# An attention kernel on one core: the threshold masks in one arithmetic form on GpSimd, and two divisions taken off VectorE's reads of PSUM

## The chip, the cores and the metric

The kernel runs on one core of one Trainium2 chip. The metric is the device time of one execution in microseconds (us). Before the change the median of three runs is 1256.25 us (1255.8 to 1259.92).

## The reference, cut to what matters

32 batches of 256 tokens with 128 channels, 16 heads of 8 channels. Each batch passes a layer norm, a query/key/value product, a layer norm of each head's queries and keys, and then two attentions, which are mixed and projected (D is 8, and topk is 12 of 256 keys):

```python
scores = jnp.einsum('bhnd,bhmd->bhnm', q, k) / jnp.sqrt(jnp.float32(D))
aw = jax.nn.softmax(scores, axis=-1)
kth = jax.lax.top_k(aw, topk)[0][..., -1:]
mask = (aw >= kth).astype(aw.dtype)
aws = aw * mask
aws = aws / (aws.sum(-1, keepdims=True) + 1e-08)
o_s = jnp.einsum('bhnm,bhmd->bhnd', aws, v)
qf = jax.nn.softmax(q, axis=-1)
kf = jax.nn.softmax(k, axis=-1)
kv = jnp.einsum('bhnd,bhne->bhde', kf, v)
z = jnp.einsum('bhnd,bhd->bhn', qf, kf.sum(axis=2))
o_l = jnp.einsum('bhnd,bhde->bhne', qf, kv) / (z[..., None] + 1e-06)
o = a * o_s + (1.0 - a) * o_l
return o @ Wproj.T + bproj
```

## The kernel before

Each engine runs its own program, written out by hand, and the engines meet only at semaphores. The loop over batches (`it`) is software-pipelined: iterations -2 to 3 and 28 to 33 are written out, and between them runs a hardware loop whose body holds four batches. In an iteration every engine goes through eight units `u_` = 0 to 7, one for each pair of heads. A unit holds four tiles of 128 queries by 256 keys.

The sparse attention of one unit passes through the engines so:

- TensorE writes the scores of unit u+1 to `score_ps` (`scores`).
- VectorE takes the 8 largest of each row (`top`, L539) and GpSimd subtracts the maximum (`drop`, L371).
- ScalarE takes the exponentials (`e`, L724, with row sums in `z`), and those of the eight largest (`e8`, L729).
- VectorE, a unit later, removes the eight largest (`rest`, L546) and takes the next eight (`next`, L552). The fourth of these is the threshold.
- Two units after that unit's scores, the mask `below` is made: by GpSimd for some of the four tiles (L393, the table `POOL_TILES` = 3, 2, 3, 4, 4, 4, 3, 2) and by ScalarE for the others (L737).
- TensorE (`turn`, L841 and L842) transposes `e` and adds `below` times -2^40 in the same PSUM tile, and ScalarE copies it through a ReLU (`kept`, L694), which leaves only what passes the threshold. TensorE multiplies with the values (`product`, L862), four heads at a time, and ScalarE copies `oT` (L746).

Once a batch there is other work in fixed units. For the linear attention TensorE multiplies in unit 2 (L958, result in `work_ps`: 32 groups of 8 sums and a divisor), and VectorE in unit 3 takes the reciprocals of the divisors (`lin_z`, L567) and the products (`lin`, L570), both from PSUM. In unit 5 TensorE turns the sparse sums of the previous batch into `pv_ps` (`sums`, L873), and VectorE makes `den` (L586), its reciprocal (L591) and `o_sparse` (L594). TensorE may write `work_ps` anew (L968) when `lin` is there, and `pv_ps` (L862 of unit 6) when `o_sparse` is there. Other once-a-batch work of VectorE: statistics (L602, L608), `kv` (L560), `d_max` (L578), `k_rec` (L611). GpSimd's: the norms of queries and keys (L336 to L358, L381), `d_sub` (L401), `k_half`, `k_quarter` and `k_sum` (L422), `k_feat` (L429).

The queries and keys of the next batch go through DRAM. ScalarE writes three bf16 parts (`part`, L708 in unit 4, L758 in units 4 and 5), SyncE stores them (L274) and loads them as `q_slots` and `k_slots` (L281). TensorE needs them for the scores of the next batch's unit 0, at the end of unit 7.

In `extra(u_, k)` of VectorE, `k` tells the place between the removals and searches of a unit.

## Time and profile before

| what | value |
|---|---|
| median of three runs | 1256.25 us |
| the profiled execution, its own time | 1254.07 us |
| its span in the trace | 1252.3 us |
| VectorE (DVE) busy | 1187.9 us, 95% |
| ScalarE (ACT) busy | 1086.6 us, 87% |
| GpSimd (POOL) busy | 1083.9 us, 87% |
| TensorE (PE) busy | 972.0 us, 78% |
| granted TensorE clock, mean | 0.959 |

Busy time is the time in which an engine had an instruction under way. Short instructions of VectorE and ScalarE overlap: the next one starts before the one ahead has ended. So what an instruction costs on a full engine is the distance from its start to the next one's start, which the timeline gives, and not its own duration. A wait stands in brackets behind the instruction that waited, with the releaser.

### The profile page before, as it was taken

What the parts mean: (1) busy time and instruction counts of PE and PEld (TensorE: products, weight loads), DVE (VectorE), ACT (ScalarE), POOL (GpSimd) and SP (SyncE); (2) the same over time, 40 slices, a digit from 0 to 9 for tenths busy, and PEclk for the clock granted to TensorE, in tenths of its full rate; (3) what the DMA queues carried; (4) which work ended last, traced back from release to release, by engine and by line L of the source; (5) the groups of instructions that cost most, each with busy time, mean ns of one, the idle gap of its engine ahead of it and who ended that gap; (6) DMA issues with size and microseconds to landing.
All of it is one profiled execution on the core that took longest, in us unless ns stands there. A gap on an engine that the chain in (4) does not pass through costs nothing.

```text
span 1252.3 us, 38772 instructions
## 1 busy us (share of the span) xinstructions
PE 972.0 (78%) x8997; PEld 655.4 (52%) x9028; DVE 1187.9 (95%) x4553; ACT 1086.6 (87%) x3626; POOL 1083.9 (87%) x1688
## 2 busy tenths in 40 slices
PE   2578788887788777877877888788868788877876
PEld 0245555555455554555545555455545555555554
DVE  7699999999899998999989999899989999999994
ACT  2498999999799997999979899799988999999984
POOL 4598999999899997999979999799988999999974
PEclk9999999899899998999989999899999998999998
DMA  2122221212221222221122221122221222222110
GB/s 61 47 73 78 81 80 40 70 57 82 83 82 43 66 69 72 82 81 54 55 59 82 82 81 51 48 69 82 82 84 36 67 63 82 81 81 71 41 52 14
DMA packets 165211, 83.45 MB, mean 67 GB/s; under 512 B 7753, under 2 KB 164943, under 8 KB 164946
## 3 DMA queue, kind: packets, MB, share of 16 engines
q1 hardware_dynamic: 164946, 80.56, 22.4%
q8 instruction: 88, 1.44, 0.5%
q14 instruction: 177, 1.45, 0.4%
HBM read 42.78 MB, written 37.75 MB: 64 GB/s over the span
## 4 chain that ended last, share of the span: by engine, by line
DVE 53%; issue 32%; DVEq 6%; PE 5%; POOL 2%; ACT 1%; SPq 0%; DMA 0%; POOLq 0%; ACTq 0%
DVE rest L546 22%; DVE top L539 18%; DVE next L552 8%; DVEq L75 5%; POOL below L393 2%; PE turn_ps L841 1%; PE pv_ps L862 1%; DVE o_sparse L594 1%; DVE lin_z L567 1%; PE turn_ps L842 1%; ACT e L724 1%; DVE stats L602 0%; DVE den L586 0%; DVE x_mv L608 0%; DVE lin L570 0%
## 5 line engine op out<-in xcount | busy, mean ns | idle before, releaser
L393 POOL TENSOR_SCALAR below<-e,next 128x256 bf16<-128x256 f32 x800 | 724.6, 922 | 0.2 <-issue 0.2
L724 ACT ACTIVATE e<-score_ps,drop 128x256 f32<-128x256 f32 x1024 | 473.2, 481 | 53.8 <-POOL drop L371 51.3
L841 PE MATMUL turn_ps<-ident,e 128*128 128x128 f32 x2048 | 406.5, 292 | 61.9 <-issue 22.4
L546 DVE MATCH_REPLACE8 rest<-e 128x256 f32<-128x256 f32 x1024 | 409.8, 402 | 0.0
L552 DVE MAX8 next<-rest 128x8 f32<-128x256 f32 x1024 | 402.9, 406 | 0.0
L539 DVE MAX8 top<-score_ps 128x8 f32<-128x256 f32 x1024 | 358.8, 408 | 31.5 <-issue 16.9
L842 PE MATMUL turn_ps<-minus_huge,below 128*128 128x128 bf16 x2048 | 383.9, 226 | 0.0
L841 PEld LDWEIGHTS turn_ps<-ident,e 128*128 128x128 f32 x2048 | 300.3, 147 | 107.2 <-issue 62.2
L694 ACT ACTIVATE kept<-turn_ps 128x1024 f32<-128x1024 f32 x256 | 267.6, 1045 | 68.1 <-PE turn_ps L842 67.8
L842 PEld LDWEIGHTS turn_ps<-minus_huge,below 128*128 128x128 bf16 x2048 | 224.9, 110 | 0.2
L724 ACT ACTIVATION_READ_ACCUMULATOR e<-score_ps,drop 128x1 f32 x1024 | 217.6, 213 | 0.0
L862 PE MATMUL pv_ps<-kept,v_aug 128*32 128x256 f32 x2048 | 145.5, 404 | 1.9 <-ACT out_sb L770 1.3
L371 POOL TENSOR_TENSOR drop<-top 128x36 f32<-128x36 f32 x256 | 62.8, 245 | 82.3 <-DVE top L539 81.7
L823 PE MATMUL score_ps<-k_slots,q_slots 64*128 64x256 bf16 x1024 | 104.7, 282 | 19.4 <-ACT e L724 11.1
L737 ACT ACTIVATE below<-e,next 128x256 bf16<-128x256 f32 x224 | 108.2, 516 | 0.0
L862 PEld LDWEIGHTS pv_ps<-kept,v_aug 128*32 128x32 f32 x2048 | 55.6, 113 | 49.5 <-issue 29.5
L823 PEld LDWEIGHTS score_ps<-k_slots,q_slots 64*128 64x128 bf16 x1024 | 31.0, 95 | 79.8 <-issue 72.8
L939 PE MATMUL work_ps<-w_qk,xnT 128*128 128x256 f32 x128 | 46.8, 448 | 31.6 <-ACT xnT L786 31.6
L546 DVE MATCH_VALUE_LOAD rest<-e 128x8 f32 x1024 | 68.4, 67 | 0.8 <-ACT e L729 0.8
L729 ACT ACTIVATE e<-drop 128x32 f32<-128x32 f32 x256 | 63.4, 248 | 0.0
L873 PE MATMUL pv_ps<-gather,oT 128*128 128x128 f32 x256 | 35.0, 280 | 29.4 <-ACT oT L746 29.2
L958 PE MATMUL work_ps<-kv,qfT 128*128 128x144 f32 x128 | 25.3, 322 | 35.1 <-DVE kv L560 35.1
(156 smaller groups left out, 1333.0 us busy)
## 6 DMA issues: line engine op xcount, KB each, us to landing
part_slots<-part SPq DMA_DIRECT2D x128, 192.0 KB, 2.3
q_slots<-part_slots SPq DMA_DIRECT2D x64, 256.0 KB, 3.4
k_slots<-part_slots SPq DMA_DIRECT2D x64, 256.0 KB, 4.0
part_slots<-part SPq DMA_DIRECT2D x64, 128.0 KB, 2.0
x_sb<-in_L_attn_x SPq DMA_DIRECT2D x32, 128.0 KB, 4.0
x_res<-in_L_attn_x SPq DMA_DIRECT2D x32, 128.0 KB, 3.9
out_y<-out_sb SPq DMA_DIRECT2D x32, 128.0 KB, 4.4
w_ops<-in_L_ffn_W SPq DMA_DIRECT2D x1, 512.0 KB
```

Of the source, the lines that this page charges most:

```text
L393: nc.gpsimd.tensor_scalar(below[:, r, t, :], e[:, r, t, :], next8[:, r, t, TOPK - 9:TOPK - 8], None, ALU.is_lt).then_inc(s["below_pool"], 1)
L539: nc.vector.max(top[:, q, t, 1:9], score_ps[:, q, t // 2, t % 2, :]).then_inc(s["top_ready"], 1)
L546: nc.vector.match_replace(rest[:, t, :], e8[:, (u_ - 1) % 2, t, :], e[:, (u_ - 1) % RING, t, :], REMOVED).then_inc(s["rest_ready"], 1)
L552: nc.vector.max(next8[:, (u_ - 1) % RING, t, :], rest[:, t, :]).then_inc(s["next_ready"], 1)
L694: nc.scalar.activation(kept[:, u_ % 4], turn_ps[:], ACT.Relu).then_inc(s["turn_copied"], 1)
L724: nc.scalar.activation(e[:, u_ % RING, t, :], score_ps[:, u_ % 2, t // 2, t % 2, :], ACT.Exp, bias=drop[:, u_ % 2, t, 0:1], accum_out=z[:, ...
L729: nc.scalar.activation(e8[:, u_ % 2], drop[:, u_ % 2, :, 1:9], ACT.Exp).then_inc(s["e8_ready"], 1)
L737: nc.scalar.activation(below[:, r, t, :], e[:, r, t, :], ACT.Relu, scale=-1.0, bias=next8[:, r, t, TOPK - 9:TOPK - 8]).then_inc(s["below_a ...
L823: last = mm(score_ps[:, v_ % 2, hh, nt, :], q_slots[rows, side, v_, nt * P:(nt + 1) * P], k_slots[rows, side, v_, :], start=True, stop=True)
L841: mm(dst, e[:, r, t, keys], ident[:], start=True, stop=False, is_transpose=True)
L842: last = mm(dst, below[:, r, t, keys], minus_huge[:], start=False, stop=True)
L862: last = mm(pv_ps[32 * j:32 * (j + 1), 0:N], v_aug[:, side, mc, 4 * q + j, :], kept[:, v_ % 4, j % 2, mc, :], start=(mc == 0), stop=(mc == ...
```

## The change

All four tiles of every unit's mask are made by GpSimd, no longer by comparing but as min(e - threshold, 0). The result is at most zero, so the matrix that TensorE multiplies it with changes its sign (`huge` for `minus_huge`). ScalarE makes no masks any more, and TensorE waits for one semaphore in place of two.

Both divisions are split in four steps. ScalarE copies the 288 columns from PSUM (`lin_raw` in unit 3, ahead of that unit's exponentials; `sums_sb` in unit 5, behind them). VectorE takes only the reciprocals, from SBUF (`lin_z` in unit 4, `den` in unit 7). GpSimd multiplies (`lin` in unit 4, `o_sparse` in unit 7) and forms the denominator of the sparse part in unit 6. TensorE may write the PSUM tiles anew once ScalarE has copied them.

```diff
-POOL_TILES = (3, 2, 3, 4, 4, 4, 3, 2)
...
+                    if u_ == 6 and exists(it - 1):
+                        wait_alone(pool, s["sums_copied"], it, s["waits_passed"])
+                        nc.gpsimd.tensor_scalar(den[:, 0], z[:, nxt].rearrange("p t h -> p (t h)"), SUM_EPS, None,
+                                                ALU.mult).then_inc(s["den_step"], 1)
+                        pool.wait_ge(s["den_step"], it)
+                        nc.gpsimd.tensor_tensor(den[:, 1], den[:, 0], sums_sb[:, :, D], ALU.add).then_inc(
+                            s["den_ready"], 1)
...
-                        for t in range(POOL_TILES[r]):
+                        for t in range(TILES):
                             wait_alone(pool, s["next_ready"], TILES * (g - 2) + t + 1, s["waits_passed"])
                             nc.gpsimd.tensor_scalar(below[:, r, t, :], e[:, r, t, :],
-                                                    next8[:, r, t, TOPK - 9:TOPK - 8], None,
-                                                    ALU.is_lt).then_inc(s["below_pool"], 1)
+                                                    next8[:, r, t, TOPK - 9:TOPK - 8], 0.0,
+                                                    ALU.subtract, ALU.min).then_inc(s["below_ready"], 1)
...
+                    if u_ == 4 and exists(it):
+                        pool.wait_ge(s["linz_ready"], it + 1)
+                        nc.gpsimd.tensor_tensor(lin[:, par].rearrange("p t (h d) -> p (t h) d", d=D),
+                                                lin_raw[:, :, 0:D],
+                                                lin_z[:].unsqueeze(2).to_broadcast([P, NT * H, D]),
+                                                ALU.mult).then_inc(s["lin_ready"], 1)
...
+                    if u_ == 7 and exists(it - 1):
+                        pool.wait_ge(s["rden_ready"], it)
+                        nc.gpsimd.tensor_tensor(o_sparse[:].rearrange("p t (h d) -> p (t h) d", d=D),
+                                                sums_sb[:, :, 0:D],
+                                                den[:, 2].unsqueeze(2).to_broadcast([P, NT * H, D]),
+                                                ALU.mult).then_inc(s["osp_ready"], 1)
...
-                    if u_ == 3 and k in (1, 3) and exists(it):
-                        w = work_ps[:, 0:NT * H * VA].rearrange("p (t h e) -> p t h e", t=NT, e=VA)
-                        if k == 1:
-                            dve.wait_ge(s["w_lin"], it + 1)
-                            nc.vector.reciprocal(lin_z[:], w[:, :, :, D]).then_inc(s["linz_step"], 1)
-                        if k == 3:
-                            dve.wait_ge(s["linz_step"], it + 1)
-                            nc.vector.tensor_tensor(
-                                lin[:, par].rearrange("p t (h d) -> p (t h) d", d=D),
-                                work_ps[:, 0:NT * H * VA].rearrange("p (g e) -> p g e", e=VA)[:, :, 0:D],
-                                lin_z[:].rearrange("p t h -> p (t h)").unsqueeze(2).to_broadcast([P, NT * H, D]),
-                                ALU.mult).then_inc(s["lin_ready"], 1)
...
-                    if u_ == 5 and 1 <= k <= 4 and exists(it - 1):
-                        w = pv_ps[:, 0:NT * H * VA].rearrange("p (g e) -> p g e", e=VA)
-                        n = 2 * (it - 1)
-                        if k == 1:
-                            dve.wait_ge(s["w_turn"], it)
-                            nc.vector.scalar_tensor_tensor(out=den[:, 0], in0=z[:, nxt].rearrange("p t h -> p (t h)"),
-                                                           scalar=SUM_EPS, in1=w[:, :, D], op0=ALU.mult,
-                                                           op1=ALU.add).then_inc(s["den_step"], 1)
-                        if k == 2:
-                            dve.wait_ge(s["den_step"], n + 1)
-                            nc.vector.reciprocal(den[:, 1], den[:, 0]).then_inc(s["den_step"], 1)
-                        if k == 4:
-                            dve.wait_ge(s["den_step"], n + 2)
-                            nc.vector.tensor_tensor(o_sparse[:].rearrange("p t (h d) -> p (t h) d", d=D), w[:, :, 0:D],
-                                                    den[:, 1].unsqueeze(2).to_broadcast([P, NT * H, D]),
-                                                    ALU.mult).then_inc(s["osp_ready"], 1)
+                    if u_ == 4 and k == 1 and exists(it):
+                        dve.wait_ge(s["lin_copied"], it + 1)
+                        nc.vector.reciprocal(lin_z[:], lin_raw[:, :, D]).then_inc(s["linz_ready"], 1)
+                    if u_ == 7 and k == 1 and exists(it - 1):
+                        dve.wait_ge(s["den_ready"], it)
+                        nc.vector.reciprocal(den[:, 2], den[:, 1]).then_inc(s["rden_ready"], 1)
...
+                    if u_ == 3 and exists(it):
+                        act.wait_ge(s["w_lin"], it + 1)
+                        wait(act, s["lin_ready"], it)
+                        nc.scalar.copy(lin_raw[:].rearrange("p g e -> p (g e)"), work_ps[:, 0:NT * H * VA]).then_inc(
+                            s["lin_copied"], 1)
...
-                        for t in range(POOL_TILES[r], TILES):
-                            nc.scalar.activation(below[:, r, t, :], e[:, r, t, :], ACT.Relu, scale=-1.0,
-                                                 bias=next8[:, r, t, TOPK - 9:TOPK - 8]).then_inc(s["below_act"], 1)
...
+                    if u_ == 5 and exists(it - 1):
+                        act.wait_ge(s["w_turn"], it)
+                        wait(act, s["osp_ready"], it - 1)
+                        nc.scalar.copy(sums_sb[:].rearrange("p g e -> p (g e)"), pv_ps[:, 0:NT * H * VA]).then_inc(
+                            s["sums_copied"], 1)
...
-                    pe.wait_ge(s["below_pool"], POOL_SUM * batch + POOL_UPTO[r + 1])
-                    wait(pe, s["below_act"], (UNITS * TILES - POOL_SUM) * batch + TILES * (r + 1) - POOL_UPTO[r + 1])
+                    pe.wait_ge(s["below_ready"], TILES * (g2 + 1))
...
-                                last = mm(dst, below[:, r, t, keys], minus_huge[:], start=False, stop=True)
+                                last = mm(dst, below[:, r, t, keys], huge[:], start=False, stop=True)
...
-                        wait(pe, s["osp_ready"], it)
+                        wait(pe, s["sums_copied"], it)
...
-                        wait(pe, s["lin_ready"], it + 1)
+                        wait(pe, s["lin_copied"], it + 1)
```

VectorE, units 3 and 4 of one iteration, before (the lines L546, L552 and L539 are the removals, the searches for the next eight and for the first eight):

```order
L539 MAX top<-score_ps 128x8 x4
L546 MATCH_REPLACE rest<-e 128x256 x2
L567 RECIPROCAL lin_z<-work_ps 128x32
L552 MAX next<-rest 128x8
L546 MATCH_REPLACE rest<-e 128x256
L570 TENSOR_TENSOR lin<-work_ps,lin_z 128x256
L552 MAX next<-rest 128x8
L546 MATCH_REPLACE rest<-e 128x256
L552 MAX next<-rest 128x8
L578 TENSOR_REDUCE d_max<-qkn 128x64
L552 MAX next<-rest 128x8
L539 MAX top<-score_ps 128x8 x4
```

The same place in the changed kernel (its line numbers are others: L560, L567 and L573 are those three):

```order
L560 MAX top<-score_ps 128x8 x4
L567 MATCH_REPLACE rest<-e 128x256 x2
L573 MAX next<-rest 128x8
L567 MATCH_REPLACE rest<-e 128x256
L573 MAX next<-rest 128x8
L567 MATCH_REPLACE rest<-e 128x256
L573 MAX next<-rest 128x8
L586 TENSOR_REDUCE d_max<-qkn 128x64
L573 MAX next<-rest 128x8
L560 MAX top<-score_ps 128x8 x4
```

The reciprocal and the product have left unit 3. One reciprocal, from SBUF, stands in unit 4, behind these rows.

GpSimd, units 6 and 7, before:

```order
L371 TENSOR_TENSOR drop<-top 128x36
L393 TENSOR_SCALAR below<-e,next 128x256 x4
L371 TENSOR_TENSOR drop<-top 128x36
L393 TENSOR_SCALAR below<-e,next 128x256 x4
L429 TENSOR_TENSOR k_feat<-k_exp,k_rec 128x256
```

And in the changed kernel:

```order
L370 TENSOR_TENSOR drop<-top 128x36
L386 TENSOR_SCALAR den<-z 128x32
L389 TENSOR_TENSOR den<-den,sums_sb 128x32
L400 TENSOR_SCALAR below<-e,next 128x256 x4
L370 TENSOR_TENSOR drop<-top 128x36
L400 TENSOR_SCALAR below<-e,next 128x256 x4
L442 TENSOR_TENSOR o_sparse<-sums_sb,den 128x256
L450 TENSOR_TENSOR k_feat<-k_exp,k_rec 128x256
```

Three instructions have come in, two of them ahead of the masks of unit 6. In these two units GpSimd made all four tiles before, too.

## Rows read from the trace of the kernel before

**Rows 1.** The page, part 1: busy time of each engine.

```profile
PE 972.0 (78%) x8997; PEld 655.4 (52%) x9028; DVE 1187.9 (95%) x4553; ACT 1086.6 (87%) x3626; POOL 1083.9 (87%) x1688
```

**Rows 2.** Busy time by stretch: PE, PEld, DVE, ACT, POOL, then clock and DMA.

```profile
100.00:300.00 200.00, 166.08 (x1560) 112.56 (x1564) 199.16 (x767) 185.94 (x622) 184.12 (x289) 0.97 0.27 76
```

**Rows 3.** Waits of VectorE: total us, times, longest.

```profile
DVE top L539 <- issue: 16.9, 5, 3.6
DVE top L539 <- PE score_ps L823: 13.6, 8, 5.7
DVE den L586 <- PE pv_ps L873: 12.6, 2, 12.0
```

**Rows 4.** Timeline of TensorE, one batch apart: start, us, what.

```profile
520.98 0.70 PE L939 MATMUL work_ps<-w_qk,xnT 128*128 128x256 f32 x2 [1.04 <-ACT xnT L786]
...
557.32 0.70 PE L939 MATMUL work_ps<-w_qk,xnT 128*128 128x256 f32 x2 [1.04 <-ACT xnT L786]
```

**Rows 5.** Timeline of VectorE in unit 3, around the linear part.

```profile
613.12 0.34 DVE L567 RECIPROCAL lin_z<-work_ps 128x32 f32<-128x32 f32 x1
613.38 0.36 DVE L552 MAX8 next<-rest 128x8 f32<-128x256 f32 x1
...
614.05 0.40 DVE L570 TENSOR_TENSOR lin<-work_ps,lin_z 128x256 f32<-128x256 f32 x1
614.38 0.41 DVE L552 MAX8 next<-rest 128x8 f32<-128x256 f32 x1
```

**Rows 6.** Timeline of VectorE in unit 5, around the sparse part.

```profile
622.66 0.17 DVE L586 SCALAR_TENSOR_TENSOR den<-z,pv_ps 128x32 f32<-128x32 f32 x1
622.76 0.41 DVE L552 MAX8 next<-rest 128x8 f32<-128x256 f32 x1
623.09 0.32 DVE L591 RECIPROCAL den<-den 128x32 f32<-128x32 f32 x1
623.35 0.02 DVE L546 MATCH_VALUE_LOAD rest<-e 128x8 f32 x1
...
624.02 0.39 DVE L594 TENSOR_TENSOR o_sparse<-pv_ps,den 128x256 f32<-128x256 f32 x1
624.34 0.07 DVE L546 MATCH_VALUE_LOAD rest<-e 128x8 f32 x1
```

**Rows 7.** Timeline of VectorE in unit 6, around a reciprocal from SBUF.

```profile
629.28 0.32 DVE L611 RECIPROCAL k_rec<-k_sum 128x32 f32<-128x32 f32 x1
629.53 0.36 DVE L552 MAX8 next<-rest 128x8 f32<-128x256 f32 x1
```

**Rows 8.** Groups of GpSimd, shapes apart: busy us, mean ns, idle before.

```profile
L393 POOL TENSOR_SCALAR below<-e,next 128x256 bf16<-128x256 f32 x800 | 724.6, 922 | 0.2 <-issue 0.2
...
L429 POOL TENSOR_TENSOR k_feat<-k_exp,k_rec 128x256 f32<-128x256 f32 x32 | 20.1, 630 | 0.5 <-DVE k_rec L611 0.5
L338 POOL TENSOR_SCALAR qk_rsqrt<-qk_rsqrt 128x64 f32<-128x64 f32 x32 | 7.9, 247 | 6.4 <-POOL qk_rsqrt L336 6.4
L412 POOL TENSOR_SCALAR x_shift<-x_shift 128x2 f32<-128x2 f32 x32 | 7.5, 235 | 6.4 <-POOL x_shift L409 6.4
L338 POOL TENSOR_SCALAR x_rsqrt<-x_rsqrt 128x2 f32<-128x2 f32 x32 | 6.1, 191 | 6.4 <-POOL x_rsqrt L336 6.4
```

**Rows 9.** Groups of ScalarE, the same columns.

```profile
L737 ACT ACTIVATE below<-e,next 128x256 bf16<-128x256 f32 x224 | 108.2, 516 | 0.0
L746 ACT COPY oT<-pv_ps 128x256 f32<-128x256 f32 x128 | 49.1, 384 | 1.7 <-PE pv_ps L862 1.7
```

**Rows 10.** Timeline, units 6 to 0: the load, the scores, VectorE's search.

```profile
592.07 0.51 SPq L281 DMA_DIRECT2D k_slots<-part_slots  x1
...
595.65 0.40 PE L823 MATMUL score_ps<-k_slots,q_slots 64*128 64x256 bf16 x4
...
597.67 1.40 DVE L539 MAX8 top<-score_ps 128x8 f32<-128x256 f32 x4
```

**Rows 11.** Timeline of GpSimd at the end: the last nine masks.

```profile
1227.80 8.10 POOL L393 TENSOR_SCALAR below<-e,next 128x256 bf16<-128x256 f32 x9
```

More of the change, by code:

```diff
@@ L57 @@
 ROWS = len(SLOTS) * D
-POOL_TILES = (3, 2, 3, 4, 4, 4, 3, 2)
-POOL_SUM = sum(POOL_TILES)
-POOL_UPTO = tuple(sum(POOL_TILES[:v]) for v in range(UNITS + 1))
 RING = 8
@@ L112, in build @@
         ident = sb("ident", [P, P])
-        minus_huge = sb("minus_huge", [P, P], BF16)
+        huge = sb("huge", [P, P], BF16)
         minus_one = sb("minus_one", [P, P], BF16)
@@ L177, in build @@
         qfT = sb("qfT", [P, N])
-        lin_z = sb("lin_z", [P, NT, H])
+        lin_raw = sb("lin_raw", [P, NT * H, VA])
+        lin_z = sb("lin_z", [P, NT * H])
         lin = sb("lin", [P, 2, NT, C])
@@ L194, in build @@
         oT = sb("oT", [P, 2, QUADS, N])
-        den = sb("den", [P, 2, NT * H])
+        sums_sb = sb("sums_sb", [P, NT * H, VA])
+        den = sb("den", [P, 3, NT * H])
         o_sparse = sb("o_sparse", [P, NT, C])
@@ L206, in build @@
             scores_ready top_ready rest_ready next_ready drop_ready e8_ready waits_passed
-            exp_done below_pool below_act turn_ready turn_copied pv_ready pv_copied
+            exp_done below_ready turn_ready turn_copied pv_ready pv_copied
             x_stats x_mean x_rsqrt_step x_rsqrt_ready x_newton xn_ready
@@ L211, in build @@
             dmax_ready dsub_ready dexp_ready ksum_step ksum_ready krec_ready feat_ready
-            w_v_ready v_copied w_kv kv_ready w_qfT qfT_copied w_lin linz_step lin_ready
-            w_turn den_step osp_ready w_osT osT_copied w_out y_ready""".split()
+            w_v_ready v_copied w_kv kv_ready w_qfT qfT_copied w_lin lin_copied linz_ready lin_ready
+            w_turn sums_copied den_step den_ready rden_ready osp_ready w_osT osT_copied w_out y_ready""".split()
         s = {n: sem(n) for n in names}
@@ L296, in _ @@
             select(ident[:], ALU.not_equal, 1.0, 0, [[-1, P]], 1, 1).then_inc(s["ident_ready"], 1)
-            nc.gpsimd.memset(minus_huge[:], 0.0).then_inc(s["pool_step"], 1)
+            nc.gpsimd.memset(huge[:], 0.0).then_inc(s["pool_step"], 1)
             nc.gpsimd.memset(own_head[:], 1.0).then_inc(s["pool_step"], 1)
@@ L301, in _ @@
             nc.gpsimd.memset(v_aug[:], 0.0).then_inc(s["pool_step"], 1)
-            select(minus_huge[:], ALU.not_equal, -HUGE, 0, [[-1, P]], 1, 4).then_inc(s["pool_const"], 1)
+            select(huge[:], ALU.not_equal, HUGE, 0, [[-1, P]], 1, 4).then_inc(s["pool_const"], 1)
             select(own_head[:], ALU.is_ge, 0.0, 0, [[-D, H], [0, VA]], 1, 4).then_inc(s["pool_step"], 1)
@@ L718, in body @@
                         if u_ == 0:
-                            wait(act, s["osp_ready"], it - 1)
+                            wait(act, s["den_ready"], it - 1)
                         wait(act, s["turn_ready"], g - RING + 1)
@@ L729, in body @@
                         nc.scalar.activation(e8[:, u_ % 2], drop[:, u_ % 2, :, 1:9], ACT.Exp).then_inc(s["e8_ready"], 1)
-                    if exists(it if u_ >= 2 else it - 1):
-                        r = (u_ - 2) % RING
-                        act.wait_ge(s["next_ready"], TILES * (g - 1))
-                        for t in range(POOL_TILES[r], TILES):
-                            nc.scalar.activation(below[:, r, t, :], e[:, r, t, :], ACT.Relu, scale=-1.0,
-                                                 bias=next8[:, r, t, TOPK - 9:TOPK - 8]).then_inc(s["below_act"], 1)
                     if u_ % 2 == 0 and exists(it if u_ >= 6 else it - 1):
@@ L830, in turn @@
                     r = (u_ - 4) % RING
-                    batch = it if u_ >= 4 else it - 1
-                    pe.wait_ge(s["below_pool"], POOL_SUM * batch + POOL_UPTO[r + 1])
-                    wait(pe, s["below_act"], (UNITS * TILES - POOL_SUM) * batch + TILES * (r + 1) - POOL_UPTO[r + 1])
+                    pe.wait_ge(s["below_ready"], TILES * (g2 + 1))
                     wait(pe, s["turn_copied"], g2)
```

## The prediction, on record before the changed kernel ran

> **What bounds the kernel now.** I read busy times first, then a stretch of the steady part, then VectorE's waits, and last the timeline between the instructions that the change touches. Over the whole span VectorE leads with 95%, and ScalarE and GpSimd follow with 87% each [rows 1]; from this alone any of the three could be the limit. The steady stretch decides: from 100 to 300 us VectorE is busy for 199.16 of 200 us, GpSimd for 184.12 and ScalarE for 185.94 [rows 2]. So in the steady part VectorE never waits, and the other two do. VectorE's list of waits says the same: in the whole execution it has three large entries, 16.9, 13.6 and 12.6 us [rows 3]. The 16.9 us are five stops of up to 3.6 us in front of the first search of a unit, in which the profile sees nothing waited for. Each lies before the first search of an iteration whose number is a multiple of four: they are the jumps back to the head of the loop. The 12.6 us are the drain after the last batch. Of the 13.6 us, 5.7 lie in one wait at the start, the others mostly just behind those jumps. A batch takes 557.32 - 520.98 = 36.3 us [rows 4], and 32 of them make 1163 of the 1252 us. Whatever shortens VectorE's program in a batch shortens the batch, as long as the others follow.
>
> **VectorE, what leaves and what comes.** VectorE's instructions overlap, so I take the distance from a start to the next start.
> - Linear part: `lin_z` 613.38 - 613.12 = 0.26 us, `lin` 614.38 - 614.05 = 0.33 us [rows 5].
> - Sparse part: `den` 622.76 - 622.66 = 0.10 us, its reciprocal 623.35 - 623.09 = 0.26 us, `o_sparse` 624.34 - 624.02 = 0.32 us [rows 6].
> - These leave: 0.26 + 0.33 + 0.10 + 0.26 + 0.32 = 1.27 us a batch.
> - Two reciprocals of 32 elements from SBUF come in. `k_rec` is exactly that, and its slot is 629.53 - 629.28 = 0.25 us [rows 7], so 0.50 us come.
>
> Net 0.77 us a batch, 32 times: 24.6 us, of which the last batch's sparse part doesn't count, since it lies in the drain. I take 24.0 us. By the instructions' own durations (0.34 + 0.40 + 0.17 + 0.32 + 0.39 less 0.64, so 0.98 us a batch) it would be 31 us, but those count overlapped time twice.
>
> **GpSimd, the unknown price.** The old mask costs 922 ns a tile [rows 8], or 8.10 / 9 = 0.90 us from start to start [rows 11]. The trace has no tile with subtract and min, so I bound it. The form with two arithmetic operations exists at 64 and at 2 elements: 247 and 191 ns [rows 8], which is (247 - 191) / 62 = 0.90 ns an element. At 256 elements that gives 191 + 254 x 0.90 = 420 ns. This is my lower bound. The upper bound is the comparison's own 922 ns: if what makes it dear is the threshold read from memory, or the bf16 output, both of which stay, nothing gets cheaper. The row with one operation (235 ns at 2 elements against 191 with two) shows that leaving out the second operation does not make an instruction cheaper [rows 8]. I take 0.45 us, near the lower end, since the two rows with the same pair form are the nearest in operation, and leave the upper end to a rival.
>
> The new work: two products of 256 elements at the 630 ns of `k_feat`, and two operations of 32 elements at some 240 ns, between the 235 and the 247 of the two small rows [rows 8]: 1.74 us a batch. All other work of GpSimd is 1083.9 - 724.6 = 359.3 us, or 11.2 us a batch [rows 1, 8]. With 32 masks at 0.45 us that is 11.2 + 1.7 + 14.4 = 27.3 us, against a batch of 36.3 - 0.8 = 35.5 us. GpSimd has room. It becomes the bound when 32 masks take more than 35.5 - 12.9 = 22.6 us, so at 0.71 us a mask.
>
> The row for the old mask works out at (922 - 191) / 254 = 2.9 ns an element, three times the pair form's [rows 8]. The Trainium skill (GPSIMD Engine Reference, section 3.1) gives bodies of at most two operations 1.03 cycles an element and a tight loop without branches some 1.8 cycles at best, and section 7 gives bodies that make a boolean 2.03 cycles unless unrolled. By its figures, at the 1.2 GHz that it states, an estimate for the new mask is 0.2 to 0.4 us plus the fixed part, so 0.4 to 0.6 us; the sum would stay as it is, since that lies under the 0.71 us that decide. The rows agree with the page on the direction, not on the comparison's size.
>
> **ScalarE.** 224 masks of 516 ns go, 108.2 us of busy time, and 64 copies of 288 columns come, at `oT`'s 384 ns for 256 columns some 0.4 us each, 26 us [rows 9]. Net 82 us less, of 1086.6 [rows 1]. It was not the bound, so this gives nothing by itself. Locally it is not all relief: in unit 5 ScalarE made no masks (all four were GpSimd's), and now the copy of `sums_sb` stands ahead of the last part cast. The copy of `lin_raw` stands ahead of the exponentials of unit 3. It waits for the product out of `kv`, which TensorE issues in unit 2, while those exponentials wait for VectorE's search in unit 3; so it should be hidden.
>
> **The new waits.** VectorE in unit 4 waits for a copy made in unit 3, and in unit 7 for a denominator that GpSimd forms near the head of unit 6. Each has about a unit of some 4.5 us (36.3 / 8) to arrive [rows 4]. Behind them on VectorE stand the searches that everything waits for, so a late one would cost in full. GpSimd's masks of unit 6 stand behind the wait for `sums_copied`, and TensorE needs these masks only two units after that. TensorE's waits for `work_ps` and `pv_ps` now end with a copy in place of the division; the one comes earlier, the other at about the same place in the unit.
>
> **Start, jumps, drain.** The stops at the jumps (16.9 us) and the waits behind them (some 7.5 us of the 13.6) [rows 3] don't come from work that the change touches, and I leave them. In the drain GpSimd's last nine masks take 8.10 us [rows 11] and would take 4 us or less, but TensorE's turns and ScalarE's copies then pace it; I give that 1 to 2 us of gain. Against it the last division becomes a chain of copy, two small operations, reciprocal and product, 0.4 + 0.5 + 0.3 + 0.6 = 1.8 us where 1.0 us stood, with two more handovers. The two cancel.
>
> **The sum.** 1254.07 - 24.0 = 1230.1 us for an execution like the profiled one. That one was 2.2 us under the median, so against the median 1256.25 - 24 = 1232 us.
>
> **Rivals.**
> - *A, VectorE stays full and the batch shrinks by 0.77 us*: 1232 us, own range 1225 to 1239. For it: 199.16 of 200 us, and a batch in which nobody else is over 93% busy. Chance 0.62.
> - *B, the mask is not cheap, and GpSimd becomes the bound* (slower). From 0.71 us a mask on. At 0.90 us a batch takes 11.2 + 1.7 + 28.8 = 41.7 us, 5.4 more than now, 32 times 173 us: about 1430 us. At 0.80 us it is 38.5 us, and 1325 us. For it: 922 ns is the only row with this size, this scalar from memory and this output; against it the slope of the pair form. Chance 0.17.
> - *C, the gain goes into a new wait*. The place to look is the round through DRAM: the last part is cast in unit 5, stored and loaded (issued at 592.07), the scores start at 595.65 and end 0.4 us later, and VectorE searches them at 597.67 [rows 10]. The margin is 1.6 us. VectorE now gets from unit 5 to unit 0 faster by 0.68 - 0.25 = 0.43 us, and the cast comes 0.35 to 0.4 us later behind the new copy. That takes half the margin. If the margin fell short by all of the 0.77 us, the time would be the old 1256 us; between, 1245 to 1256. Chance 0.12.
> - *D, more than the sum*: shorter queues on GpSimd and ScalarE also shorten the waits behind the jumps and the start, by up to those 7.5 us and the drain's 2 us [rows 3]: 1216 to 1224 us. Chance 0.09.
>
> The Trainium skill (GPSIMD Engine Reference, section 4.1) advises against GpSimd for elementwise work, which it puts at about half VectorE's speed with two inputs. The rows agree on the ratio's direction: 630 ns for `k_feat` against 0.33 us for the `lin` slot [rows 5, 8]. Alone it would speak against the move; it counts only on an engine without room, and then it is rival B.
>
> **How the numbers follow.** The likeliest is A, 1232 us. The range from 1216 to 1256 holds A, C and D, 0.83 together; B lies outside. About 0.3% (3.8 us) is what a measurement of this kernel can tell from no change. Faster than that are A, D and a part of C (0.04): 0.75. Within it, the rest of C less a little: 0.07. Slower: B, and 0.01 of C: 0.18.
>
> **What would show it.** Right if a batch lasts some 35.5 us and VectorE is still busy for over 99% of the steady stretch, with its busy total some 24 to 31 us lower; if the mask group on GpSimd has a mean under 0.6 us and GpSimd falls to some 70%; if the five stops at the jumps stay. Wrong if the waits of VectorE list new entries at the reciprocals or at the searches of unit 0, or if GpSimd's masks have TensorE's turns and then the searches wait.

## The result: 1654 us, a third slower

The changed kernel takes 1654.2 us (median of 4 runs, 1653.39 to 1655.17) against 1256.03 us (1253.92 to 1259.92): a ratio of 1.317, 95% interval [1.313, 1.320]. The prediction was 1232 us.

The page of the changed kernel, part 1, and its stretch from 100 to 300 us (the columns of [rows 1, 2]):

```profile
PE 1173.5 (71%) x8997; PEld 773.1 (47%) x9028; DVE 1195.5 (72%) x4457; ACT 1032.3 (62%) x3466; POOL 1558.8 (94%) x2040
100.00:300.00 200.00, 144.17 (x1121) 94.81 (x1122) 147.08 (x550) 128.42 (x431) 194.36 (x253) 0.80 0.18 51
```

VectorE has fallen from 199.16 to 147.08 of 200 us [rows 2], and GpSimd leads with 194.36. The other engines follow. TensorE is busy for 144.17 of the 200 us in place of 166.08 [rows 2], and its granted clock is 0.80 on average in place of 0.97, so it spends part of the time at the lower of its two levels (1.2 of 2.4 GHz). GpSimd's group for the masks stands at the head of part 5 of the page:

```profile
L400 POOL TENSOR_SCALAR below<-e,next 128x256 bf16<-128x256 f32 x1024 | 1151.3, 1146 | 0.0
```

That is 1146 ns a mask where the comparison took 922 ns [rows 8], and 1024 of them where there were 800. The batch and the way in which GpSimd holds up the others, in timelines: VectorE (two rows, one batch apart), then GpSimd, then ScalarE and VectorE together:

```profile
708.92 0.69 DVE L586 TENSOR_REDUCE d_max<-qkn 128x64 f32<-128x512 f32 x1 [2.16 <-POOL qkn L357]
...
758.84 0.69 DVE L586 TENSOR_REDUCE d_max<-qkn 128x64 f32<-128x512 f32 x1 [2.17 <-POOL qkn L357]
```

```profile
719.43 0.19 POOL L337 TENSOR_SCALAR x_rsqrt<-x_rsqrt 128x2 f32<-128x2 f32 x1 [0.20 <-POOL x_rsqrt L335]
...
720.58 0.63 POOL L424 TENSOR_TENSOR lin<-lin_raw,lin_z 128x256 f32<-128x256 f32 x1
721.16 0.24 POOL L370 TENSOR_TENSOR drop<-top 128x36 f32<-128x36 f32 x1
721.39 4.50 POOL L400 TENSOR_SCALAR below<-e,next 128x256 bf16<-128x256 f32 x4
```

```profile
719.76 1.41 DVE L560 MAX8 top<-score_ps 128x8 f32<-128x256 f32 x4
721.44 0.47 ACT L728 ACTIVATE e<-score_ps,drop 128x256 f32<-128x256 f32 x1 [2.47 <-POOL drop L370]
723.67 0.09 DVE L567 MATCH_VALUE_LOAD rest<-e 128x8 f32 x1 [2.50 <-ACT e L733]
```

A batch takes 758.84 - 708.92 = 49.9 us instead of 36.3 [rows 4]. `drop`, a small subtraction, stands in GpSimd's queue behind masks and products; ScalarE's exponentials wait for it, and VectorE's removals for the exponentials. The waits in sum (us, times, longest), ScalarE's in the first row:

```profile
ACT e L728 <- POOL drop L370: 392.6, 217, 4.0
DVE rest L567 <- ACT e L733: 273.2, 198, 2.5
DVE d_max L586 <- POOL qkn L357: 66.1, 31, 2.3
DVE top L560 <- issue: 22.3, 6, 4.9
```

In the chain that ended last (part 4 of the page) the masks alone have nearly half:

```profile
POOL below L400 46%; POOL drop L370 3%; ACT e L728 3%; POOLq L72 2%; POOL qkn L357 2%; POOL d_sub L408 2%; DVE rest L567 2%; DVE top L560 2%; POOL sq_half L380 1%; POOL o_sparse L442 1%; PE pv_ps L859 1%; POOL k_feat L450 1%; DVE next L573 1%; POOL k_half L436 1%; POOL sq_quarter L380 1%
```

### The profile page after: what moved, and what is told of

Same layout as the page of the kernel before. It is cut to its first block, busy times and chain, and to the rows that moved or that the text cites. A ratio compares the mean times of both kernels' runs of the same rounds, so it can differ in the third digit from the quotient of the medians.

```text
span 1653.0 us, 38768 instructions
## 1 busy us (share of the span) xinstructions
PE 1173.5 (71%) x8997; PEld 773.1 (47%) x9028; DVE 1195.5 (72%) x4457; ACT 1032.3 (62%) x3466; POOL 1558.8 (94%) x2040
## 3 DMA queue, kind: packets, MB, share of 16 engines
q1 hardware_dynamic: 164946, 80.56, 16.9%
## 4 chain that ended last, share of the span: by engine, by line
POOL 61%; issue 23%; DVE 5%; ACT 3%; PE 3%; POOLq 3%; DMA 1%; DVEq 1%; SPq 0%; ACTq 0%
POOL below L400 46%; POOL drop L370 3%; ACT e L728 3%; POOLq L72 2%; POOL qkn L357 2%; POOL d_sub L408 2%; DVE rest L567 2%; DVE top L560 2%; POOL sq_half L380 1%; POOL o_sparse L442 1%; PE pv_ps L859 1%; POOL k_feat L450 1%; DVE next L573 1%; POOL k_half L436 1%; POOL sq_quarter L380 1%
## 5 line engine op out<-in xcount | busy, mean ns | idle before, releaser
L400 POOL TENSOR_SCALAR below<-e,next 128x256 bf16<-128x256 f32 x1024 | 1151.3, 1146 | 0.0
L838 PE MATMUL turn_ps<-ident,e 128*128 128x128 f32 x2048 | 484.9, 329 | 101.3 <-POOL below L400 89.8
L839 PE MATMUL turn_ps<-huge,below 128*128 128x128 bf16 x2048 | 453.3, 250 | 0.0
L838 PEld LDWEIGHTS turn_ps<-ident,e 128*128 128x128 f32 x2048 | 347.3, 170 | 175.2 <-POOL below L400 89.7
L567 DVE MATCH_REPLACE8 rest<-e 128x256 f32<-128x256 f32 x1024 | 415.0, 408 | 0.0
L573 DVE MAX8 next<-rest 128x8 f32<-128x256 f32 x1024 | 407.4, 411 | 0.6
L560 DVE MAX8 top<-score_ps 128x8 f32<-128x256 f32 x1024 | 361.3, 415 | 55.5 <-PE score_ps L822 32.4
L567 DVE MATCH_VALUE_LOAD rest<-e 128x8 f32 x1024 | 79.9, 78 | 274.0 <-ACT e L733 273.2
L839 PEld LDWEIGHTS turn_ps<-huge,below 128*128 128x128 bf16 x2048 | 251.2, 123 | 0.7
L859 PE MATMUL pv_ps<-kept,v_aug 128*32 128x256 f32 x2048 | 175.0, 470 | 92.0 <-ACT sums_sb L747 90.8
L909 PE MATMUL pv_ps<-x_res,ident 128*128 128x128 f32 x128 | 32.8, 344 | 79.6 <-issue 79.2
L370 POOL TENSOR_TENSOR drop<-top 128x36 f32<-128x36 f32 x256 | 63.9, 250 | 12.3 <-DVE top L560 12.3
L965 PE MATMUL work_ps<-ident,qkn 128*128 128x128 f32 x128 | 31.6, 395 | 54.0 <-POOL qkn L357 53.9
L586 DVE TENSOR_REDUCE d_max<-qkn 128x64 f32<-128x512 f32 x32 | 21.9, 685 | 66.1 <-POOL qkn L357 66.1
L909 PEld LDWEIGHTS pv_ps<-x_res,ident 128*128 128x128 f32 x128 | 23.4, 228 | 86.6 <-issue 85.7
```

Of the source, the lines that this page charges most:

```text
L370: nc.gpsimd.tensor_tensor(drop[:, q], top[:, q], top[:, q, :, 1:2].to_broadcast([P, TILES, 9]), ALU.subtract).then_inc(s["drop_ready"], 1)
L400: nc.gpsimd.tensor_scalar(below[:, r, t, :], e[:, r, t, :], next8[:, r, t, TOPK - 9:TOPK - 8], 0.0, ALU.subtract, ALU.min).then_inc(s["bel ...
L560: nc.vector.max(top[:, q, t, 1:9], score_ps[:, q, t // 2, t % 2, :]).then_inc(s["top_ready"], 1)
L567: nc.vector.match_replace(rest[:, t, :], e8[:, (u_ - 1) % 2, t, :], e[:, (u_ - 1) % RING, t, :], REMOVED).then_inc(s["rest_ready"], 1)
L573: nc.vector.max(next8[:, (u_ - 1) % RING, t, :], rest[:, t, :]).then_inc(s["next_ready"], 1)
L838: mm(dst, e[:, r, t, keys], ident[:], start=True, stop=False, is_transpose=True)
```

## Experiments

The theory after the result: (1) min(e - threshold, 0) is a dear form on GpSimd, and (2) with all masks there, GpSimd paces the batch. Rivals: what makes it dear is the bf16 output or the threshold in memory; the divisions' new waits do a part of it. Later there was a second question: where VectorE's 24 us went.

**1. What a form costs (m1_forms, m2_forms).** The kernel before, with further instructions of GpSimd behind its last batch, four of each form; their results aren't used. Each of the two ran once. In m1_forms:

```diff
+            def f_pair_memory_bf16(i):
+                return nc.gpsimd.tensor_scalar(probe_b[:, i, :], one, thr, 0.0, ALU.subtract, ALU.min)
...
+            def f_multadd_memory_f32(i):
+                return nc.gpsimd.tensor_scalar(probe_f[:, i, :], one, thr, 1.5, ALU.mult, ALU.add)
```

> The kernel before, and behind its last mask GpSimd runs 14 forms of instruction, four times each (one of them on 1024 elements, three on shorter rows). Known: comparison with the threshold from memory, bf16 out: 922 ns; subtract and min with the threshold from memory: 1146 ns. Theory 1, the scalar from memory is what costs: with an immediate both fall to 420 to 500 ns, and multiply-add with a scalar from memory rises to 900 to 1150. Theory 2, the bf16 output costs: with f32 out both fall under 600 ns. Theory 3, the number and kind of operations cost, whatever the operands: subtract and min stays at 1100 to 1150 in every variant, one operation (comparison, min, subtract) at 900 to 950. Theory 4, only the small rows misled me (a fixed part hides the elements at 64): multiply-add with immediates at 256 elements is itself at 900 or more, and a 64-element subtract and min takes 250 to 400. The two-input subtract of 256 elements should take the 630 ns of k_feat.

GpSimd's timeline: the comparison (bf16 output; with a constant as threshold; with f32 output), the pair subtract and min (the same three), mult and add with constants and with the scalar from memory, min alone, subtract and min on 64 elements, and the subtraction of two tensors (the second is the threshold, repeated along the row):

```profile
1236.70 3.61 POOL L443 TENSOR_SCALAR probe_b<-e,next 128x256 bf16<-128x256 f32 x4
1240.40 3.29 POOL L445 TENSOR_SCALAR probe_b<-e 128x256 bf16<-128x256 f32 x4
1243.79 3.62 POOL L447 TENSOR_SCALAR probe_f<-e,next 128x256 f32<-128x256 f32 x4
1247.50 4.49 POOL L449 TENSOR_SCALAR probe_b<-e,next 128x256 bf16<-128x256 f32 x4
1252.08 4.16 POOL L451 TENSOR_SCALAR probe_b<-e 128x256 bf16<-128x256 f32 x4
1256.34 4.49 POOL L453 TENSOR_SCALAR probe_f<-e,next 128x256 f32<-128x256 f32 x4
...
1264.63 1.51 POOL L457 TENSOR_SCALAR probe_f<-e 128x256 f32<-128x256 f32 x4
1266.24 1.84 POOL L459 TENSOR_SCALAR probe_f<-e,next 128x256 f32<-128x256 f32 x4
1268.18 3.61 POOL L461 TENSOR_SCALAR probe_b<-e,next 128x256 bf16<-128x256 f32 x4
1271.88 1.92 POOL L463 TENSOR_SCALAR probe_b<-e,next 128x64 bf16<-128x64 f32 x4
...
1275.65 2.32 POOL L467 TENSOR_TENSOR probe_b<-e,next 128x256 bf16<-128x256 f32 x4
```

The output's type makes no difference (3.61 and 3.62 us for four, 4.49 and 4.49). A scalar from memory costs (3.61 - 3.29) / 4 = 0.08 us. The operations decide: comparison or min alone 0.90 us, subtract with min 4.49 / 4 = 1.12 us, mult with add 0.38 us with constants and 0.46 us with the scalar from memory. So theory 3 of what was expected comes closest. The slope that the prediction took from mult and add fits that pair (it gave 420 ns at 256 elements) and not the mask's. The size was not what misled: already at 64 elements subtract with min takes 1.92 / 4 = 0.48 us, where mult with add, with constants, has 247 ns [rows 8].

m2_forms asks how far the cheap form reaches, with 13 more, all at 256 elements, f32, scalar from memory:

```diff
+            def f_mult_add(i):
+                return nc.gpsimd.tensor_scalar(probe[:, i, :], one, thr, 0.0, ALU.mult, ALU.add)
...
+            def f_add_min(i):
+                return nc.gpsimd.tensor_scalar(probe[:, i, :], one, thr, 0.5, ALU.add, ALU.min)
```

> The kernel before, and behind its last mask 13 more forms of GpSimd's tensor-scalar instruction on 256 elements in f32, four times each, all with the first scalar from memory. From the run before: multiply then add 0.46 us from start to start, one operation (comparison, min or subtract) 0.90, subtract then min 1.12. Theory 1, only a pair is fast and min, subtract and comparison are slow operations: the pairs of add and mult are all at 0.46, and mult alone and add alone too. Theory 2, only the sequence multiply then add has the fast form: all other pairs are at 1.0 to 1.15 and all single operations at 0.90, mult alone too. Theory 3, the speed depends on the first operation: every pair that begins with mult is at 0.46, mult then min and mult then less among them, which would give a cheap mask.

The timeline: mult with add, mult alone, add with mult, add with add, mult with mult, mult with min, add with min:

```profile
1234.69 1.85 POOL L440 TENSOR_SCALAR probe<-e,next 128x256 f32<-128x256 f32 x4
1236.64 3.64 POOL L446 TENSOR_SCALAR probe<-e,next 128x256 f32<-128x256 f32 x4
...
1244.11 1.85 POOL L458 TENSOR_SCALAR probe<-e,next 128x256 f32<-128x256 f32 x4
1246.05 4.52 POOL L464 TENSOR_SCALAR probe<-e,next 128x256 f32<-128x256 f32 x4
1250.66 1.85 POOL L470 TENSOR_SCALAR probe<-e,next 128x256 f32<-128x256 f32 x4
...
1261.84 4.51 POOL L488 TENSOR_SCALAR probe<-e,next 128x256 f32<-128x256 f32 x4
1266.43 4.50 POOL L494 TENSOR_SCALAR probe<-e,next 128x256 f32<-128x256 f32 x4
```

Three of the pairs, (mult, add), (add, mult) and (mult, mult), take 0.46 us; each of the seven other pairs takes 1.13 us; a single operation takes 0.91 us, even mult. So one operation costs twice what a cheap pair does, and none of the three theories holds whole. Of the forms with one tensor that ran, none that clamps or compares is cheap. A comparison of two tensors was not run; the subtraction of two tensors, at 2.32 / 4 = 0.58 us, is cheaper than the old mask, so that way to a cheaper mask is open.

**2. The mask's form alone, and the count alone (e1_mask_form, e3_compare_all).** e1 is the kernel before, with the new form for GpSimd's 25 tiles and the other sign of the matrix for them:

```diff
-                                                    next8[:, r, t, TOPK - 9:TOPK - 8], None,
-                                                    ALU.is_lt).then_inc(s["below_pool"], 1)
+                                                    next8[:, r, t, TOPK - 9:TOPK - 8], 0.0,
+                                                    ALU.subtract, ALU.min).then_inc(s["below_pool"], 1)
```

> The kernel before with only the form of GpSimd's masks changed (25 of 32 tiles a batch, as before; ScalarE keeps its 7; the divisions are as before). If the price of the form is the cause: GpSimd then has 11.2 + 25 x 1.115 = 39.1 us of work a batch against VectorE's 36.3, so 1330 to 1360 us. If the cause lay in the moved divisions and their waits, it stays at 1256.

1358.09 us (1354.14 to 1364.62), ratio 1.082 [1.079, 1.086]. This lies within the 1330 to 1360 us expected if the price of the form is the cause, at their slow end. The form alone costs 102 us, with 25 masks of 1140 ns on GpSimd.

e3 is the changed kernel with the comparison in place of the pair, for all 32 tiles, and the matrix's old sign:

```diff
-                                                    next8[:, r, t, TOPK - 9:TOPK - 8], 0.0,
-                                                    ALU.subtract, ALU.min).then_inc(s["below_ready"], 1)
+                                                    next8[:, r, t, TOPK - 9:TOPK - 8], None,
+                                                    ALU.is_lt).then_inc(s["below_ready"], 1)
```

> The change with the comparison in place of subtract and min, all four tiles still on GpSimd. If GpSimd's work alone sets the time, it is 1654 less 1024 x (1.115 - 0.90) = 220 us: 1434, between 1425 and 1450. If a chain of waits through GpSimd's queue adds to it, it is above 1450.

1442.88 us (1442.09 to 1443.43), ratio 1.148 [1.146, 1.150], as expected of GpSimd's work alone. Of the 398 us, 1654.2 - 1442.9 = 211 are the dearer form in 32 tiles, and 187 remain with the old form.

The batches settle the arithmetic. By the median distance from one `d_max` to the next, a batch takes 40.17 us in e1, 42.97 in e3, 49.91 in the changed kernel. Less the masks (25 x 1.115, 32 x 0.90, 32 x 1.115) that leaves 12.3, 14.2 and 14.2 us. GpSimd's other work takes 12.3 us of a batch, and 14.2 with the divisions, not 11.2 and 12.9. The 1.1 to 1.3 us between are pauses between small steps that depend on each other, and no busy time has them: in a batch of the changed kernel three of 0.20 us, as at 719.43 above, and ten of 0.08 us, 1.4 us together; in e1, without the divisions, 1.2 us.

**3. The divisions alone (e2_divisions_only).** The changed kernel, with the masks of before (25 comparisons on GpSimd, 7 on ScalarE).

```diff
+POOL_TILES = (3, 2, 3, 4, 4, 4, 3, 2)
...
-                        for t in range(TILES):
+                        for t in range(POOL_TILES[r]):
```

> The change with the masks as before (25 tiles compared by GpSimd, 7 made by ScalarE); only the divisions are moved. If my term for VectorE is right (0.77 us a batch) and GpSimd, with 11.2 + 1.8 + 25 x 0.90 = 35.5 us against 35.5 of VectorE, just keeps up: 1230 to 1243 us, with a ratio under 0.995. If the new waits eat the gain: 1250 to 1270.

Missed on the slow side: 1276.2 us (1274.13 to 1279.0), ratio 1.016 [1.013, 1.018]. New waits of VectorE:

```profile
DVE top L563 <- PE score_ps L834: 30.5, 26, 5.8
...
DVE rest L570 <- ACT e L736: 14.5, 32, 0.9
```

By the numbers of experiment 2, GpSimd needs 25 x 0.90 + 14.2 = 36.7 us a batch, where VectorE needs 35.6; the median batch of e2 takes 37.0 us. So GpSimd's work is more than VectorE's already here. Experiment 5 tests whether that is the whole of it.

**4. The divisions with room on GpSimd (e4_cheap_stub, e6_cheap_stub_old_divisions).** Both put mult with add in the place of the mask's operations, for all 32 tiles on GpSimd. That is no threshold: with it the kernel leaves out the sparse attention. e4 has the new divisions, e6 the old ones.

```diff
-                                                    ALU.subtract, ALU.min).then_inc(s["below_ready"], 1)
+                                                    ALU.mult, ALU.add).then_inc(s["below_ready"], 1)
```

> The change, with a mask instruction of the cheap form (e times the threshold, plus 0) in place of subtract and min, with the factor minus 2^40 behind it: it has the size, operands and output of a mask and takes 0.46 us, but masks everything away, so the sparse part of the result is left out. This is the price that my prediction took (0.45 us). If everything else in it was right, VectorE is the bound again and a batch takes 36.35 - 0.77 = 35.6 us: 1228 to 1238 us. If the moved divisions bring waits of their own on VectorE, it stays above 1245.

> The kernel before with all 32 masks of a batch on GpSimd in the cheap form of the stub (the sparse part of the result is left out here too), and the divisions as before, on VectorE. VectorE's program is that of before, so a batch takes 36.35 us and the kernel 1250 to 1257 us. The difference to the stub with the divisions moved is what moving them is worth when nobody else is full: 24 us by my sum.

e4 takes 1246.07 us (1241.9 to 1246.66), ratio 0.992 [0.990, 0.994]; e6 1252.31 us (1249.44 to 1259.11), ratio 0.997 [0.996, 0.999]. A mask takes 482 ns in e4, close to what the prediction had assumed, and still e4 lies above the 1228 to 1238 us expected of it. e6 came as expected, but only 6.2 us lie between the two, not 24, and 10 between e4 and the kernel before. So even with a mask at the assumed price this change does not reach 1232 us. e4 still has the late copy, which the next experiment takes up.

**5. A version that computes all and leaves room (e5_copy_early_23, e9_23_tiles_copy_late).** e5 is e2 with 23 comparisons on GpSimd (23 x 0.90 + 14.2 = 34.9 us) and ScalarE's copy of the sparse sums ahead of unit 5's exponentials. e9 has only the first of the two edits. (In the diff the copy's block moves within ScalarE's unit, the rest of its lines with it.)

```diff
-POOL_TILES = (3, 2, 3, 4, 4, 4, 3, 2)
+POOL_TILES = (3, 2, 3, 3, 4, 3, 3, 2)
...
+                    if u_ == 5 and exists(it - 1):
+                        act.wait_ge(s["w_turn"], it)
...
-                    if u_ == 5 and exists(it - 1):
-                        act.wait_ge(s["w_turn"], it)
```

> The run with only the divisions moved, with 23 tiles compared by GpSimd a batch in place of 25 (9 made by ScalarE), and the copy of the sparse sums ahead of unit 5's exponentials. GpSimd then needs 23 x 0.90 + 14.1 = 34.8 us a batch, under VectorE's 35.6. If GpSimd's saturation is what ate the gain of the divisions (it needed 25 x 0.90 + 14.1 = 36.6 there): 1232 to 1245 us. If ScalarE, with two more masks, or the handovers are the new bound: 1250 to 1275.

> e2_divisions_only with 23 tiles of masks on GpSimd instead of 25, and the copy of the value sums left at the end of unit 5. It parts the two edits of e5_copy_early_23. If GpSimd's budget was all that e2 lacked (25 x 0.90 + 14.1 = 36.6 us against a batch of 35.6; with 23 it is 34.8), this kernel takes e5's time, 1243 to 1249 us. If the late copy, for which TensorE waits 24.7 us in sum, was the cause, it stays at 1260 us or more.

e5 takes 1245.07 us (1243.51 to 1245.48), at the slow end of what was expected, ratio 0.991 [0.989, 0.993]; e9 1251.6 us (1246.62 to 1256.15), ratio 0.996 [0.994, 0.998]. Two tiles fewer give 24.6 us, the early copy 6.5 more: neither theory of e9 was whole. These timelines around unit 7's search, e9 first and then e5, show how the copy acts through the load from DRAM:

```profile
555.72 1.40 DVE L563 MAX8 top<-score_ps 128x8 f32<-128x256 f32 x4
556.49 0.36 SPq L283 DMA_DIRECT2D q_slots<-part_slots  x1
...
557.99 0.51 SPq L283 DMA_DIRECT2D k_slots<-part_slots  x1
...
560.54 0.40 PE L834 MATMUL score_ps<-k_slots,q_slots 64*128 64x256 bf16 x4 [1.15 <-ACT e L731]
...
561.08 1.42 DVE L563 MAX8 top<-score_ps 128x8 f32<-128x256 f32 x4 [0.68 <-PE score_ps L834]
```

```profile
585.61 0.36 SPq L283 DMA_DIRECT2D q_slots<-part_slots  x1
...
586.17 1.40 DVE L563 MAX8 top<-score_ps 128x8 f32<-128x256 f32 x4
...
587.12 0.51 SPq L283 DMA_DIRECT2D k_slots<-part_slots  x1
...
589.61 0.40 PE L834 MATMUL score_ps<-k_slots,q_slots 64*128 64x256 bf16 x4 [0.40 <-DMA k_slots<-part_slots]
...
590.58 1.41 DVE L563 MAX8 top<-score_ps 128x8 f32<-128x256 f32 x4
```

In e9 the last load is issued 2.27 us behind the search, in e5 0.95 us. In both the scores of the next batch start some 2.5 us behind that issue, and only e9's next search has to wait for them. (The trace puts e9's wait at 560.54 down to an exponential; in e5 it names the load.)

**6. Where the rest of the 24 us is (e8_before_trips12, e7_early_trips12, e10_no_loop).** VectorE's first searches divide its program into units. The median unit, over the 30 batches between the first and the last, is shorter in e5 in just the places forecast: unit 3 by 5.34 - 4.80 us, unit 5 by 4.84 - 4.21, and longer in units 4 and 7, where a reciprocal came, by 0.20 and 0.21. The eight medians sum to 36.36 us before and 35.61 in e5. Not in the medians are the units around the jumps back to the loop's head. Before, around 630 us, and then e5:

```profile
629.81 1.39 DVE L539 MAX8 top<-score_ps 128x8 f32<-128x256 f32 x4
637.62 1.43 DVE L539 MAX8 top<-score_ps 128x8 f32<-128x256 f32 x4 [3.53 <-issue]
643.77 1.43 DVE L539 MAX8 top<-score_ps 128x8 f32<-128x256 f32 x4 [1.85 <-PE score_ps L823]
```

```profile
621.76 1.40 DVE L563 MAX8 top<-score_ps 128x8 f32<-128x256 f32 x4
629.85 1.42 DVE L563 MAX8 top<-score_ps 128x8 f32<-128x256 f32 x4 [3.60 <-issue]
637.72 1.43 DVE L563 MAX8 top<-score_ps 128x8 f32<-128x256 f32 x4 [3.57 <-PE score_ps L834]
```

Units 7 and 0 take 13.96 us before and 15.96 in e5. All that units last beyond their medians sums to 27.2 us before, 41.2 in e4, 36.3 in e5 (each good to about half a us, since 30 times the medians' last digit enters). Most of it, 24.6 us before and 33.6 in e5, lies in units 7 and 0 around the five jumps.

There is more to such a jump than the stop. Stretches of 4 us around the same places, before and then e5 (PE, PEld, DVE, ACT, POOL, clock and DMA as in [rows 2]):

```profile
636.00:640.00 4.00, 1.77 (x11) 1.47 (x12) 2.38 (x9) 0.00 (x0) 0.77 (x2) 0.50 0.05 12
640.00:644.00 4.00, 4.00 (x34) 1.90 (x34) 2.15 (x9) 2.92 (x11) 3.55 (x6) 0.64 0.01 2
```

```profile
628.00:632.00 4.00, 0.07 (x1) 0.08 (x2) 2.15 (x9) 0.00 (x0) 0.63 (x3) 0.50 0.31 79
632.00:636.00 4.00, 4.00 (x32) 2.53 (x32) 2.15 (x9) 1.22 (x2) 3.78 (x6) 0.50 0.02 6
```

TensorE is nearly idle in the stop, its granted clock falls to 0.50, the lower level, and behind the stop it is busy for 4.00 of 4.00 us while the clock is still at 0.64 and at 0.50. There VectorE waits for its scores, 1.85 us before and 3.57 in e5.

To test whether the jumps are the cause, the hardware loop goes over 12 batches a trip instead of 4, in the kernel before (e8) and in e5 (e7), and isn't there at all in e10 (e5 with all batches written out):

```diff
-            with engine.Fori(first, last - 3, XRING) as i:
-                for j in range(XRING):
-                    body(i + j, j % 2, j)
+            with engine.Fori(first, last - 11, 3 * XRING) as i:
+                for j in range(3 * XRING):
+                    body(i + j, j % 2, j % XRING)
```

> The kernel before, its hardware loop going over 12 batches a trip (two trips, one jump back) instead of 4 (six trips, five jumps back). In the trace of the kernel before, units 7 and 0 around each of the five jumps are together about 5.2 us longer than the same units elsewhere. If the jumps cause that, four jumps fewer save about 21 us: 1233 to 1240 us. Rival: the long units come from something else that recurs every four batches, such as the x_sb ring and its loads; then 1252 to 1258 us.

> The divisions on GpSimd and ScalarE with 23 tiles of masks on GpSimd and the early copy (e5_copy_early_23), in trips of 12 batches. There each of the five jumps stretches units 7 and 0 by about 7.0 us. If VectorE's relief of 0.77 us a batch is whole and the jumps take it back, this kernel saves 28 us by four jumps fewer: 1214 to 1221 us, 15 to 20 us under the kernel before in trips of 12 (instead of the 11 us between the two in trips of 4). Rival: the relief is lost elsewhere; then the distance between the two stays at 11 us.

> e7_early_trips12 with no hardware loop at all: the 24 batches are written out. The one jump left in e7 stretches two units by 6.0 us together. If the jump alone does that, this kernel takes 1211 to 1215 us. If a trip's end and start cost nothing by themselves and the first fetch of longer code is what costs, it stays at 1218 us or gets slower.

Each ratio is to the runs of the kernel before that were made beside it.

| kernel | median us (runs) | ratio [95% interval] | units beyond their medians, us |
|---|---|---|---|
| before, trips of 4 | 1255.15 (1253.67 to 1257.76) | 1 | 27.2 |
| e8, before, trips of 12 | 1238.64 (1234.67 to 1240.47) | 0.986 [0.983, 0.988] | 12.4 |
| e5, trips of 4 | 1245.07 (1243.51 to 1245.48) | 0.991 [0.989, 0.993] | 36.3 |
| e7, e5 in trips of 12 | 1218.58 (1216.9 to 1220.74) | 0.971 [0.969, 0.972] | 10.0 |
| e10, e5 without a loop | 1209.41 (1207.49 to 1216.64) | 0.966 [0.963, 0.969] | 1.8 |

e8 and e7 came as expected, e10 1.6 us under its range. VectorE's waits in e10 have no "issue" entry before the searches any more:

```profile
DVE den L597 <- POOL den L391: 12.4, 1, 12.4
DVE top L562 <- PE score_ps L833: 7.4, 5, 5.7
```

Four jumps fewer save 16.5 us in the kernel before, 4.1 each, and 26.5 us in e5, 6.6 each. With rare jumps e5's edits gain 1238.6 - 1218.6 = 20 us, close to the 24 forecast; with a jump in every fourth batch, 11. e10 is the fastest of all, 3.4% under the kernel before. The Trainium skill (Runtime: NRT & Kernel Launch, section on instruction fetch mechanics) says that a taken branch whose target lies outside the fetched window stops the engine until the target has come, and that this is one reason why kernels prefer to be unrolled. The runs agree that unrolling pays, 35.7 us from e5 to e10 for five jumps; that the stop is such a fetch, no run here shows.

## Why the prediction was wrong

- **The step that failed is GpSimd's unknown price**: "the nearest in operation". The slope between the rows of 2 and 64 elements belonged to mult with add, and was laid on subtract with min as if all pairs were one. The mask took 1.12 us from start to start, not 0.45, and lay above even the upper bound of 0.92: "nothing gets cheaper" overlooked that it could get dearer. The rows gave no reason to exclude that. One of them hinted at it: the 235 ns on 2 elements is mult alone, the 191 ns mult with add [rows 8], and in experiment 1 mult alone takes twice as long as mult with add. So GpSimd had no room, and the batch went by its 49.9 us and not by VectorE's 35.6.
- **The Trainium skill** (GPSIMD Engine Reference, section 3.1): the estimate of 0.4 to 0.6 us made from it fits mult with add with the scalar from memory, measured at 0.46 us, and of the other pairs that ran only (add, mult) and (mult, mult). The measurement decides.
- **The decisive point of 0.71 us** was a little high: with 14.2 us of other work it lies at (35.6 - 14.2) / 32 = 0.67 us. GpSimd's 11.2 + 1.7 us left out the pauses between dependent steps.
- **Rival B** was the right mechanism. It had 1430 us for a price of 0.90 us, and e3, which has that price, takes 1442.9 us. At 1.12 us, with the 14.2 us that e3 leaves for the rest, a batch is 35.7 + 14.2 = 49.9 us, as measured. The batch is 13.57 us longer; 32 times that is 434 us, and the result is 398 us over. What is left of the span beside 32 batches shrank from 1252.3 - 32 x 36.34 = 89 to 1653.0 - 32 x 49.91 = 56 us.
- **VectorE's net 0.77 us** was right: the medians of e5's units give 36.36 - 35.61 = 0.75 us, unit by unit where it was said, and its busy total there is 1164.4 us, 23.5 less than before.
- **"I leave them"**, of the stops at the jumps, was wrong in size. In e5 the units beyond their medians take 9.1 us more than before. Half of that is in the stops (21.4 us in place of the 16.9 of [rows 3]), and 4.4 us are in the unit behind each (11.8 in place of 7.4), where TensorE is still at the lower clock. Why the stops themselves grow with the divisions moved is open.
- **"The two cancel"**, of the drain, was off too. From unit 7's last search to the end e5 takes 30.3 us (1213.0 to 1243.3), the kernel before 26.4. Relief 22.5 (30 batches of 0.75), less 9.1 for the jumps and 3.9 for the drain, leaves 9.5 us, and the two spans are 9.0 apart.
- **The new waits**: those at the reciprocals never appeared in VectorE's list, but for the drain. The round through DRAM (rival C) did, in e9: 6.5 us for the late copy.
- **ScalarE** had its relief, 1086.6 to 1032.3 us [rows 1]: 54 us and not 82. The sum used the rows' own durations, and those count the overlap of neighbours twice, which the prediction had minded for VectorE and not here. e6, with neither masks nor copies on ScalarE, has 1001.5 us, 85 less and not 108, and e4, with the copies, 1018.0. The rest of the way to 1032.3 us goes with the waits of the changed kernel; that waiting instructions overlap less is likely, and not shown. The relief was worth nothing, as forecast.

## What to carry to other kernels

An elementwise operation on GpSimd is priced by measuring exactly its pair of operations: a row of another pair, even of the same instruction, doesn't bound it, above or below. Before work is moved to an engine, add its pauses between dependent steps to its busy time, and ask which small instruction that others wait for will stand behind the moved work. When a sum that is right unit by unit doesn't arrive in the total, list the units that last beyond their median; here that led to the loop's jumps, worth more than the change.

## What was not expected of the hardware

- GpSimd's one-input instruction with a scalar, 256 elements: (mult, add), (add, mult) and (mult, mult) 0.46 us, a single operation 0.91 us, seven other pairs 1.13 us. Doing less, mult alone, takes twice as long as mult with add.
- Its subtraction of two tensors, 256 elements, takes 2.32 / 4 = 0.58 us, half of what the pair with a scalar takes.
- A jump back to the loop's head, on all engines, costs this kernel 4 to 7 us: 4.1 us each by the runs before with four jumps fewer, 6.6 in e5. Without any jump all units together last 1.8 us beyond their medians.
- The granted clock of TensorE falls to 0.50 in such a stop, and for some us behind it TensorE is full at the lower level (busy 4.00 of 4.00 us at a clock of 0.50), with VectorE waiting.
